# Moving the gelu's table load on ScalarE to the front of the step, in a Swin block with a depthwise convolution

## The reference, cut to what matters

```
x: (16, 112, 112, 96) float32, 7x7 windows, shifted by 3, 3 heads of 32
xn   = layer_norm(x);  roll by (-3, -3), cut into windows
q, k, v = xn @ qkv_w + qkv_b;  q = q * 32**-0.5
attn = softmax(q k^T + bias + mask)
x    = x + roll_back((attn @ v) @ proj_w + proj_b)
y    = gelu(layer_norm(x) @ fc1_w + fc1_b) @ fc2_w + fc2_b      # tanh form of gelu, hidden 384
x    = x + y
y    = relu(x);  depthwise 3x3 convolution;  1x1 convolution 96 -> 96;  batch norm by stored moments
```

## Time and profile before

| | |
|---|---|
| time, median of 3 runs | 6512.81 us (6512.4 to 6515.14) |
| time of the profiled execution | 6517.97 us |
| its span, first to last instruction | 6516.1 us |
| mean granted TensorE clock | 0.997 |
| busy in the span | PE 89%, DVE 85%, ACT 82%, POOL 58% |

### The profile page before, as it was taken

One profiled execution on the slowest core, in us unless ns is written; L12 is line 12 of the kernel. 1 busy time (PEld: TensorE's weight loads), 2 busy tenths in 40 slices (PEclk: granted clock), 3 DMA queues, 4 the chain that ended last, 5 costly groups with the idle time before them and its releaser, 6 DMA issues.

```text
span 6516.1 us, 202567 instructions
## 1 busy us (share of the span) xinstructions
PE 5792.5 (89%) x81170; PEld 4049.6 (62%) x81170; DVE 5509.5 (85%) x13747; ACT 5348.5 (82%) x11040; POOL 3807.6 (58%) x4105
## 2 busy tenths in 40 slices
PE   6889898888989888988898989888889898988887
PEld 4666666666666666666666666666666666666665
DVE  4888888888888888888888888888888888888887
ACT  5888888888888888888888888888888888888886
POOL 3655555556565655555656565555565656565563
PEclk9999999999999999999999999999999999999998
DMA  0010101010101010101010101010101010110100
GB/s 21 24 28 24 28 24 28 24 28 24 28 24 28 24 28 24 28 24 28 24 28 24 28 24 28 24 28 25 28 24 28 25 27 26 26 26 26 26 26 20
DMA packets 250521, 167.92 MB, mean 26 GB/s; under 512 B 220423, under 2 KB 220920, under 8 KB 249592
## 3 DMA queue, kind: packets, MB, share of 16 engines
q1 hardware_dynamic: 249592, 154.97, 9.2%
HBM read 77.81 MB, written 77.07 MB: 24 GB/s over the span
## 4 chain that ended last, share of the span: by engine, by line
PE 31%; POOL 24%; ACT 18%; DVE 17%; issue 10%; SPq 1%; DVEq 0%; DMA 0%; ACTq 0%; POOLq 0%
POOL prob L857 12%; PE bank L425 8%; ACT hT L564 7%; POOL rstd L863 6%; PE bank L457 5%; DVE stats L767 5%; ACT L508 5%; PE bank L374 5%; POOL x1n L873 4%; PE bank L357 4%; DVE x L803 4%; PE bank L442 3%; PE bank L469 3%; PE bank L410 3%; DVE ssum L727 2%
## 5 line engine op out<-in xcount | busy, mean ns | idle before, releaser
L751 DVE SCALAR_TENSOR_TENSOR acc<-ymap,taps,acc 96x784 f32<-96x784 f32 (+2 forms) x2176 | 2557.0, 1180 | 45.7
L863 POOL TENSOR_TENSOR rstd<-var_eps,minus_half 112x7 f32<-112x7 f32 x512 | 937.1, 1830 | 2378.1 <-DVE var_eps L782 2378.1
L374 PE MATMUL bank<-x1T,w 96*128 96x448 f32 (+1 forms) x3072 | 1143.6, 509 | 97.6 <-ACT hT L564 95.7
L393 PE MATMUL bank<-hT,w 128*96 128x448 f32 (+1 forms) x3072 | 1095.5, 492 | 0.0
L857 POOL TENSOR_TENSOR prob<-prob,srec 128x392 f32<-128x392 f32 x768 | 811.9, 1087 | 212.6 <-DVE srec L729 211.5
L374 PEld LDWEIGHTS bank<-x1T,w 96*128 96x128 f32 x3072 | 541.7, 189 | 565.7 <-issue 463.8
L873 POOL TENSOR_SCALAR xn<-x_in,minus_mean,rstd 112x96 f32<-112x96 f32 x768 | 844.8, 1111 | 0.0
L564 ACT ACTIVATE hT<-bank,bfc 128x448 f32<-128x448 f32 (+1 forms) x1536 | 824.6, 576 | 14.6 <-PE bank L374 2.2
L848 POOL TENSOR_TENSOR prob<-prob,smax 128x392 f32<-128x392 f32 x768 | 804.1, 1077 | 20.8 <-DVE smax L720 20.8
L727 DVE TENSOR_REDUCE ssum<-prob 128x8 f32<-128x392 f32 x768 | 403.9, 526 | 391.0 <-ACT prob L508 391.0
L410 PE MATMUL bank<-ident,prob 113*113 113x113 f32 x3072 | 476.6, 278 | 243.2 <-POOL prob L857 236.5
(11 more groups left out here) (88 smaller groups left out, 11065.6 us busy)
## 6 DMA issues: line engine op xcount, KB each, us to landing
out<-o_tile SPq DMA_DIRECT2D x256, 210.0 KB, 2.5
x_in<-in_x SPq DMA_DIRECT2D x256, 168.0 KB, 2.9
x_in<-in_x SPq DMA_DIRECT2D x256, 126.0 KB, 3.3
out<-o_tile SPq DMA_DIRECT2D x256, 84.0 KB, 2.5
hT<-in_L_conv_rel_bias SPq DMA_DIRECT2D x49, 0.6 KB
x1T<-in_L_conv_fc_w SPq DMA_DIRECT2D x1, 144.0 KB, 2.5
w<-in_L_conv_fc_w SPq DMA_DIRECT2D x1, 144.0 KB, 2.3
hT<-in_L_conv_qkv_w SPq DMA_DIRECT2D x1, 108.0 KB, 2.1
```

Source lines behind the costliest of these rows:

```text
L374: pe.matmul(bank[(5, 6, 0)[m]][:, 0:n * PT_], w1[:, m * 128:(m + 1) * 128], x1T[:, first * PT_:(first + n) * PT_], start=True, stop=True). ...
L393: mm = pe.matmul(bank[b][0:C, 0:n * PT_], w2[:, m, :], hT[:, m, first * PT_:(first + n) * PT_], start=False, stop=(m == MC - 1))
L751: last = dve.scalar_tensor_tensor(out=dst, in0=src, scalar=taps[:, i:i + 1], in1=dst, op0=ALU.mult, op1=ALU.add)
L863: pool.tensor_tensor(b["rstd"][:], b["var_eps"][:], minus_half[0:PT_], ALU.pow)\
```

## The change

The activation of one element that brings the load of the gelu's table stands no longer at the head of `gelus`, behind the copies to `x1T` and the first output copy, but at the head of ACT's `step`, ahead of the queries. It is issued in the same steps as before.

```diff
@@ -555,7 +555,6 @@
                 if not has(t - 1):
                     return
 
-                act.activation(table_load[:, 1:2], table_load[:, 0:1], ACT.Gelu_apprx_tanh)
                 wait(act, y_psum, nth(t - 2, 2, 1))
                 for i in range(2 * MC):
                     half, m = i // MC, i % MC
@@ -621,6 +620,8 @@
                 last.then_inc(ymap_ready, 1)
 
             def step(t, phase):
+                if has(t - 1):
+                    act.activation(table_load[:, 1:2], table_load[:, 0:1], ACT.Gelu_apprx_tanh)
                 queries(t)
                 keys(t, 0)
                 keys(t, 1)
```

## The result

| | before | with the change |
|---|---|---|
| median | 6512.60 us | 6364.14 us |
| lowest to highest | 6511.83 to 6515.14 | 6361.79 to 6366.19 |
| profiled execution | 6517.97 us | 6366.19 us |

The ratio is 0.9771 with a 95% interval of 0.9754 to 0.9788, so the kernel is 2.3% faster: 148 us, where 138 were forecast (6375 us, range 6355 to 6420).

The account below looks back on a forecast made before the run. A loop through several engines was taken to set the time, with no engine full. 236 steps x 0.61 = 144 us gained, less 15 x 0.4 = 6 us lost, gave 6512.81 - 138 = 6375 us, range 6355 to 6420.

Parts of the forecast that it names:

- The load was on the chain, and PE bounds what it is worth: ACT's load ahead of the first gelu stalls PE's matmuls; moving it gains 0.61 us per stalled step (ends 0.38, 1.42).
- The step t = 3: Early step with no output copy ahead of the load; PE's twelve matmuls take 4.22 us, against 4.84 later.
- The new place costs nothing: Ahead of the queries, the load's 1.42 us fit ACT's 1.49 us wait for PE; cost 0 us, ends 0 and 1.42.
- the rival: The load isn't hidden ahead of the queries; each step is 0.75 us longer, 6701 us; chance 0.05.
- The drain of the page: Skill's rule of 2.66 us per table switch; slot some 2.8 us, kernel slower at some 6660 us; contained in 0.05.
- The 15 steps behind an image's end: `divide` can't come earlier and taps run longer beside POOL; 0.4 us lost each (0 to 0.75), 6 us in all.
- The sum: Whole kernel: 236 x 0.61 = 144 us gained, 15 x 0.4 = 6 us lost, 138 us in all.

## Why the prediction was right, point by point

**The load was on the chain, and PE bounds what it is worth.** Right. The stage lost 0.61 us of a slot of 1.42, and PE's twelve matmuls run in one piece. The step t = 3 of the kernel before, which the estimate was read from, was a true copy of what came: 4.22 us of matmuls, `divide` at 15.44 against 15.43, L873's end at 21.99 against 21.98. The load one place earlier gives a third point on the same line.

**The new place costs nothing.** Right, but the cover was mis-sized: not 0.07 + 0.06 us but 0.81. I had counted the gap ahead of the queries and the 0.06 us between the keys and `x1n`, and not the gaps inside the pairs, which are waits for PE too. So the 0 us held with more room than I had given reasons for. The point from which the rival would have won was thus a slot of 1.42 + 0.81 + 0.61 = 2.8 us, not 2.2. With the load where nothing covers it the rival's mechanism is real, and its price of 1.36 us a step was measured to within 3 us in 341.

**The drain of the page.** The Trainium skill, "ScalarE: Activation LUTs", section "What ACT_TABLE_LOAD costs", puts a switch at 1283 ns of load and some 1380 ns of drain. The load's mean is 1283 ns here as well, 1.28 us in every row. The drain is in none: the next activation starts 0.01 us behind the load, and three switches in a row stand 1.51 us apart.

**The 15 steps behind an image's end.** This step of the prediction failed, at a small price. I said that `divide` can't come earlier there and that the taps, moved forward, would cost 0.4 us. They went from 24.49 to 24.37 us (median of the 15). POOL and DVE in the step t = 33 of the changed kernel:

```profile
875.74 0.21 POOL L867 TENSOR_TENSOR offset<-minus_mean,rstd 112x7 f32<-112x7 f32 x1
875.90 2.46 POOL L858 TENSOR_TENSOR prob<-prob,srec 128x392 f32<-128x392 f32 x3
876.63 7.49 DVE L752 SCALAR_TENSOR_TENSOR acc<-ymap,taps,acc 96x560 f32<-96x560 f32 x10
```

`divide` had been waiting for DVE's reciprocal in these steps as well, and POOL's root ended only 0.06 us ahead of it, which looked like the cause; it now starts 0.10 us earlier in its step. And the tap comes up in its first part, so it takes 2.46 us and not 2.96, and ends 0.60 us earlier. The columns of `xn` end 0.07 us later than before, 21.92 us behind `add_x`, since they now lie beside the taps throughout. The step is still 0.12 us shorter, because the projection had started from a standstill and no longer does: in the chain its first eight matmuls took 1.01 us before and take 0.80 now. The term of the sum was 15 x 0.4 = 6 us lost, and what was measured is 15 x 0.12 = 2 us gained, 8 us apart. It made the forecast too low and couldn't change its direction.

**The sum.** Between the two profiled executions the 250 steps in the middle account for 147.3 us (6258.2 and 6110.9), of 151.8 in the spans. The forecast gain was 138; 8 us of the difference are the 15 steps. The spans differ by another 4.5 us in the start: the first of these 250 steps begins at 155.2 us before and at 150.7 after. Before that point, in the first step with queries shown here, PE's four matmuls for them take 2.93 us before and 1.56 after.

```profile
83.89 2.93 PE L323 MATMUL bank<-xT,wqkv 96*96 96x392 f32 x4
```

```profile
81.51 1.56 PE L323 MATMUL bank<-xT,wqkv 96*96 96x392 f32 x4
```

That looks like the lower clock at work, but the clock's rows don't show it: from 80 to 105 us both profiles have 1.00, and from 60 to 80 us the kernel before has 1.00 and the changed one 0.58. I take the 4.5 us as chance, from one profile each, since the profiled execution before was 5.4 us above the median; it was not tried whether they stay.

## What to carry to other kernels

A load on the chain of work is worth the wait that it causes on the engine behind it, not its own length; look for a step of the same run in which that wait is missing, and read the gain there. To hide it, put it where its engine waits for another one, and count the waits inside the groups that follow as cover too: here they made 0.74 of the 0.81 us. An instruction that is put back on one engine can cost more than its length: where it lengthens a standstill of TensorE, see what the granted clock does.

## What the runs showed of the hardware

- A wait of 1.29 us on PE in each step, on top of those that were there, took the mean granted clock from 0.993 to 0.926 and cost 455 us. Twelve useless transposes in that wait took it to 0.997 and gave 457 us back.
- Between POOL and DVE the order of arrival decides. A tap of DVE (two inputs in SBUF) that came up during the first of three multiplications on POOL waited for all three, 2.46 us; one that came up during the second went ahead of the third, 3.19 us. So a `divide` that started 0.60 us later ended 0.12 us sooner.
- A table load waits for the end of the activation ahead of it and holds the next one up until its own end, 1.28 us, and nothing beyond was seen.
